# Adding up the routed expert rows: six weighted VectorE additions per token tile against ScalarE weighting and one VectorE sum

## What is computed

```python
x = x + attention(xn, Wq, bq, Wk, bk, Wv, bv, Wo, bo) + moe(xn, ...)

# attention: 16 heads of 128, causal, softmax in float32
# moe: 64 experts of capacity 128, each token goes to TOPK = 6 of them
scores = sigmoid(x_flat @ w_gate)
_, topk_idx = top_k(scores, 6)
w = take(scores, topk_idx); w = w / w.sum(-1)
out_r = (silu(g_r) * v_r) @ w_down          # per expert and slot
y_ts = out_r[flat_e, pos_c]                 # six rows of 256 per token
routed = (y_ts.reshape(N, 6, 256) * w[:, :, None]).sum(axis=1)
```

## Time and profile before

| | before |
|---|---|
| median of 3 runs | 2060.81 us (2058.49 to 2063.56) |
| the profiled execution, its own time | 2065.55 us |
| its span | 2063.8 us |
| PE busy | 1683.7 us, 82% of the span, 19016 instructions |
| DVE busy | 1502.6 us, 73%, 3148 instructions |
| ACT busy | 1090.3 us, 53%, 2300 instructions |
| POOL busy | 1101.2 us, 53%, 920 instructions |
| mean busy share of the 16 DMA engines in the slices of the attention parts | 5 to 7 tenths |

### The profile page before, as it was taken

The page is one execution under the profiler, slowest core; times in us unless marked ns, Lnnn a source line. Parts: engine busy times, 40 slices in busy tenths (PEclk is TensorE's granted clock), DMA queues, the critical chain, the costliest instruction groups (busy, mean ns, idle before and its releaser), DMA issues. The chain is left out here.

```text
span 2063.8 us, 49196 instructions
## 1 busy us (share of the span) xinstructions
PE 1683.7 (82%) x19016; PEld 1307.4 (63%) x19016; DVE 1502.6 (73%) x3148; ACT 1090.3 (53%) x2300; POOL 1101.2 (53%) x920
## 2 busy tenths in 40 slices
PE   1253089999999999999967788899899999888887
PEld 1242067777777777777756666677666666666665
DVE  5598956666667676666634478888888888888875
ACT  1520056666666666666622265555555555555564
POOL 0510046666666666666620066666666666666543
PEclk9676589999999999999977599999999999999999
DMA  5225067777665666656657566667666676667655
GB/s 182 102 102 196 0 129 135 134 136 129 123 110 104 123 103 101 105 103 104 109 130 218 171 112 121 119 120 147 120 122 121 117 139 120 122 119 144 118 90 109
DMA packets 695996, 253.35 MB, mean 123 GB/s; under 512 B 642384, under 2 KB 682145, under 8 KB 695008
## 3 DMA queue, kind: packets, MB, share of 16 engines
q1 hardware_dynamic: 668096, 204.12, 52.7%
q0 software_dynamic: 19232, 37.84, 7.2%
q10 hardware_dynamic: 8448, 8.39, 1.2%
HBM read 61.30 MB, written 54.66 MB: 56 GB/s over the span
## 5 line engine op out<-in xcount | busy, mean ns | idle before, releaser
L448 POOL TENSOR_TENSOR prob<-prob 128x128 f16<-128x128 f32 (+7 forms) x512 | 673.5, 1316 | 809.0 <-ACT prob L784 805.7
L777 ACT ACTIVATE prob<-prob,nmax 128x128 f32<-128x128 f32 (+7 forms) x512 | 398.0, 777 | 625.4 <-DVE prob L1135 568.0
L601 PE MATMUL ps_s<-kT,qT 128*128 128x512 f16 (+3 forms) x2304 | 460.6, 328 | 9.2 <-DVE prob L1135 5.7
L616 PE MATMUL ps_o<-probT,vh 128*128 128x256 f16 (+1 forms) x3840 | 434.4, 267 | 4.9 <-DMA probT<-prob 4.9
L1135 DVE TENSOR_SCALAR_CACHE_REDUCE prob<-ps_s,neg_scale 128x128 f32<-128x128 f32 (+7 forms) x512 | 408.8, 808 | 2.0 <-PE ps_s L603 1.8
L616 PEld LDWEIGHTS ps_o<-probT,vh 128*128 128x128 f16 x3840 | 372.0, 100 | 52.7 <-issue 5.8
L784 ACT CAST prob<-prob 128x128 f16<-128x128 f32 (+7 forms) x512 | 341.3, 667 | 2.9 <-DMA probT<-prob 0.6
L627 PE MATMUL ps_y<-wo,oT 128*128 128x256 f16 x1536 | 212.3, 275 | 126.5 <-DVE oT L1150 115.8
L601 PEld LDWEIGHTS ps_s<-kT,qT 128*128 128x128 f16 x2304 | 201.7, 99 | 162.9 <-issue 19.6
L567 PE MATMUL ps_t<-xT,wq 128*128 128x64 f16 x6144 | 195.2, 194 | 62.4 <-DMA xT<-xn_columns 61.0
L627 PEld LDWEIGHTS ps_y<-wo,oT 128*128 128x128 f16 x1536 | 136.2, 98 | 165.3 <-DVE oT L1150 136.7
(11 more groups left out here) (182 smaller groups left out, 1713.5 us busy)
## 6 DMA issues: line engine op xcount, KB each, us to landing
dispatched<-zeros SPq DMA_DIRECT2D x16, 512.0 KB, 5.4
probT<-prob SPq DMA_TRANSPOSE x512
ex<-dispatched SPq DMA_DIRECT2D x16, 512.0 KB, 4.3
expert_out<-eo ACTq DMA_DIRECT2D x16, 512.0 KB, 3.8
resid<-in_L_attn_x_dram SPq DMA_DIRECT2D x2, 2048.0 KB, 11.2
xn_rows<-xn SPq DMA_DIRECT2D x8, 512.0 KB, 3.0
xn_columns<-xnth SPq DMA_DIRECT2D x16, 256.0 KB, 2.3
xT<-xn_columns SPq DMA_DIRECT2D x8, 512.0 KB, 5.8
```

The lines of the kernel that those rows point to most:

```text
L448: pool.tensor_tensor(low_cols(j), prob_cols(j).rearrange("p (r k) -> p r k", k=P), high_cols(j), ALU.subtract).then_inc(p_low, 1)
L601: pe.matmul(s_cols(j, lo, hi), qT[:, u, a, j * P:(j + 1) * P], kT[:, u, c, lo:hi], start=(n == 0), stop=(n == 2 and hi < w))
L616: mm = pe.matmul(ps_o[:, lo:2 * P], vh[:, u, a, r * D:(r + 1) * D], probT[:, PT_AT[c] + 2 * r + s, lo:], start=(r + n == 0), stop=(r == 2 ...
L777: nc.scalar.activation(prob_cols(j), prob_cols(j), ACT.Exp, bias=nmax[:, j:j + 1], scale=-1.0, accum_out=rsum[:, i % 2, j:j + 1]).then_inc ...
```

## The change

The work of a tile is divided otherwise. `got` has a seventh row per buffer, which holds `cvec` and is written once. ACT multiplies each of the six gathered rows in place by its gate weight, two rows at a place, in three consecutive slots that begin 9 after the tile's first gather, each pair right after `softmax_exp`. DVE adds up the seven rows of the tile in one `tensor_reduce` over a view that has the rows innermost (slot 12 after the first gather), and adds the sum to `resid` at the next place. The gathers of tile `t` wait for the sum of tile `t - 2`, once per tile.

```diff
-        got = sb("got", [P, 2, TOPK, C])
+        got = sb("got", [P, 2, TOPK + 1, C])
+        mixed_rows = sb("mixed_rows", [P, C])
...
-        MIX_LAG = 12
+        RHYTHM = TOPK + 1
+
+        def tile_at(s, lag):
+            t, k = divmod(s - lag, RHYTHM)
+            return (t, k) if 0 <= t < NT else (-1, k)
+
...
             def gather(t, k):
-                if t > 1:
-                    pool.wait_ge(mix_step, (TOPK + 1) * (t - 2) + k + 1)
+                if t > 1 and k == 0:
+                    pool.wait_ge(mix_sum, t - 1)
...
+            def scale_rows(s):
+                t, n = tile_at(s, RHYTHM + 2)
+                if t < 0 or n > 2:
+                    return
+                if n == 0:
+                    act.wait_ge(gathered[t % 2], 16 * TOPK * (t // 2 + 1))
+                for k in (2 * n, 2 * n + 1):
+                    nc.scalar.activation(got[:, t % 2, k, :], got[:, t % 2, k, :], ACT.Copy,
+                                         scale=gate_w[:, t, k:k + 1]).then_inc(got_scaled, 1)
+
...
                     softmax_exp(i, 1)
+                    if mixing:
+                        scale_rows(TB * (i - i0) + 1)
                     high_v(i, 0)
...
-            def mix(t, k, added):
-                if k == 0:
-                    dve.wait_ge(gathered[t % 2], 16 * TOPK * (t // 2 + 1))
-                if t + k:
-                    dve.wait_ge(mix_step, (TOPK + 1) * t + k)
-                dve.wait_ge(y_added, added)
-                if k < TOPK:
-                    V.scalar_tensor_tensor(out=resid[:, t, :], in0=got[:, t % 2, k, :], scalar=gate_w[:, t, k:k + 1], in1=resid[:, t, :],
-                                           op0=ALU.mult, op1=ALU.add).then_inc(mix_step, 1)
-                else:
-                    V.tensor_tensor(resid[:, t, :], resid[:, t, :], cvec[:], ALU.add).then_inc(mix_step, 1)
+            def mix(s, added):
+                t, n = tile_at(s, RHYTHM + 5)
+                if t >= 0 and n == 0:
+                    dve.wait_ge(got_scaled, TOPK * (t + 1))
+                    if t:
+                        dve.wait_ge(mix_added, t)
+                    V.tensor_reduce(mixed_rows[:], got[:, t % 2, :, :].rearrange("p k c -> p c k"), AX.X, ALU.add).then_inc(mix_sum, 1)
+                if t >= 0 and n == 1:
+                    dve.wait_ge(mix_sum, t + 1)
+                    dve.wait_ge(y_added, added)
+                    V.tensor_tensor(resid[:, t, :], resid[:, t, :], mixed_rows[:], ALU.add).then_inc(mix_added, 1)
...
             attention(0, SPLIT, False)
+            dve.wait_ge(cvec_ready, 1)
+            for u in range(2):
+                V.tensor_copy(got[:, u, TOPK, :], cvec[:]).then_inc(bias_rows, 1)
+            dve.wait_ge(bias_rows, 2)
```

More of the change, by code:

```diff
@@ L475, in _ @@
                     low_probs(i, j)
-                    t, k = divmod(TB * (i - SPLIT) + j, TOPK + 1)
-                    if t < NT and k < TOPK:
+                    t, k = tile_at(TB * (i - SPLIT) + j, 0)
+                    if t >= 0 and k < TOPK:
                         gather(t, k)
@@ L805, in high_o, with attention @@
                 nc.scalar.activation(oT[:, c % 2, 0, :], ps_o[:, 0:2 * P], ACT.Copy, scale=O_SHIFT).then_inc(o_high, 1)
-            def attention(i0, i1):
+            def scale_rows(s):
[7 more added lines that the diff above has]
+                                         scale=gate_w[:, t, k:k + 1]).then_inc(got_scaled, 1)
+            def attention(i0, i1, mixing):
                 high_q(i0, 0)
@@ L816, in attention @@
                     softmax_exp(i, 0)
+                    if mixing:
+                        scale_rows(TB * (i - i0) + 0)
                     if old:
@@ L824, in attention @@
                     softmax_exp(i, 2)
+                    if mixing:
+                        scale_rows(TB * (i - i0) + 2)
                     if old:
@@ L828, in attention @@
                     softmax_exp(i, 3)
+                    if mixing:
+                        scale_rows(TB * (i - i0) + 3)
                     high_probs(i, 3)
                     softmax_exp(i, 4)
+                    if mixing:
+                        scale_rows(TB * (i - i0) + 4)
                     if more:
@@ L838, in attention @@
                     softmax_exp(i, 5)
+                    if mixing:
+                        scale_rows(TB * (i - i0) + 5)
                     if more:
@@ L842, in attention @@
                     softmax_exp(i, 6)
+                    if mixing:
+                        scale_rows(TB * (i - i0) + 6)
                     high_o(i, 0)
@@ L845, in attention @@
                     softmax_exp(i, 7)
+                    if mixing:
+                        scale_rows(TB * (i - i0) + 7)
                 high_probs(i1 - 1, 7)
@@ L850, in _ @@
             act.wait_ge(wscale_step, WSTEPS)
-            attention(0, SPLIT)
+            attention(0, SPLIT, False)
             def experts(g, first):
@@ L884, in _ @@
                 experts(g, False)
-            attention(SPLIT, B * H)
+            act.wait_ge(route_ready, 2)
+            attention(SPLIT, B * H, True)
         @block.vector
@@ L1187, in mix_at @@
                     def mix_at(j):
-                        n = TB * (i - i0) + j - MIX_LAG
-                        if mixing and 0 <= n < NT * (TOPK + 1):
-                            mix(n // (TOPK + 1), n % (TOPK + 1), NC * (i - 1) + j // 2)
+                        if mixing:
+                            mix(TB * (i - i0) + j, NC * (i - 1) + j // 2)
                     def mixed(j):
-                        return max(0, min(NT * (TOPK + 1), TB * (i - i0) + j - MIX_LAG + 1)) if mixing else 0
+                        return max(0, min(NT, (TB * (i - i0) + j - RHYTHM - 6) // RHYTHM + 1)) if mixing else 0
                     block_max(i, 0)
```

12 lines of the change are left out of this document (7 added, 5 removed).

## The result

| | before | after |
|---|---|---|
| median of 4 runs | 2059.74 us (2058.49 to 2063.56) | 2162.07 us (2160.3 to 2166.49) |
| the profiled execution, its own time | 2065.55 us | 2162.97 us |
| its span | 2063.8 us | 2161.2 us |

The ratio is 1.0497, with a 95% interval of 1.0475 to 1.0519: the change makes the kernel 102 us slower. The forecast was 89 us slower, 2150 with a range of 2100 to 2185, so the sign came as predicted and the time lies in the range.

What follows compares the result with a forecast made beforehand. A chain handed between DVE and ACT was taken as the bound. Per cycle of eight tiles 10.4 + 32.2 + 3.4 = 46.0 us against 23.8 removed, +22.2, times 4: 2060.8 + 89 = 2150 us, range 2100 to 2185.

Steps and rivals of the forecast that it cites:

- The chain: Second half of attention: DVE and ACT hand block_max, exponential, high and low part back and forth, some 24.0 us a step.
- the rival by which total work decides: Mixing steps: DVE's busy time decides, not its waits; steps fall to 24.3 us, 85 us less, 1975 us; chance 0.08.
- The 0.3 us that were taken off the quiet step for PE: Step without mixing: without PE's delays the chain takes some 24.0 us, 24.31 less 0.3.
- Removed, 23.8 us per cycle: Old mixing on DVE, held `yscale` included: 7 steps x 3.4 us saved per cycle of eight tiles; 4 cycles.
- The pairs on ACT, 10.4 per cycle: First and second weighted pair of a tile, ahead of the high part: 5.2 us each per cycle of eight tiles.
- The sum, 3.2 us: The seven-row sum on DVE: 2.02 us dense plus 1792 x 0.65 ns for the long step in the view.
- a free step (2.02): The strided sum on DVE takes only 2.02 us: 38 us less, 2112 us; chance 0.2.
- a full second pass (3.9): Every element of the sum takes a second 1.04 ns, 3.9 us: 22 us more, 2172 us; chance 0.12.
- What the sum waits for: DVE's sum waits for ACT's third pair behind block_max; wait and sum less present idle, 32.2 us per eight tiles.
- POOL holding the sum: DVE's sum is held by POOL's subtraction as `yscale` was: 16 us more, 2166 us; chance 0.06.
- The addition, 3.4 per cycle: Adding the sum to `resid` on DVE, once at each place per eight tiles, costs one step's present mixing, 3.4 us.
- the clock rival: PE: longer stalls bring twice as much lower-clock time, as much as now on the chain: 22 us more, 2172; chance 0.06.

Runs made afterwards that it cites:

- the bare kernel: The changed kernel with no mixing at all (no weighting, sum or additions; the gathers stay): 1991.05 us, 0.9649 of the kernel before.
- the two halves: The changed kernel with ScalarE's weighting alone, 2042.29 us, and with the sum and its addition alone, rows unweighted, 2063.36 us.
- the kernel with both edits: The changed kernel with the sum one place later and reading neighbouring floats (wrong elements added up): 2087.96 us, 1.0115 of the kernel before.
- the fastest version: The kernel before with six weighted additions per tile on DVE at chosen places, none ahead of `yscale`, constant row added in the first half: 1985.97 us.

## Why the prediction came right, and where its sizes were off

*The chain.* It held. The step without mixing and gathers takes 24.29 us with DVE at 69% and ACT at 65% of the stretch, and the rival by which total work decides (1975 us) fell: DVE lost work, and the step became 3.5 us longer. The 0.3 us that were taken off the quiet step for PE are there as waits, without mixing and gathers (1195 to 1980 us; in total, times, longest),

```profile
ACT oT L810 <- PE ps_o L621: 17.4, 34, 7.1
```

that is 0.3 us each but for the longest, but no run has a step under 24.29 except the last one, which has less to do. Since "before" and "after" were reckoned from the same 24.0, this cancels. How near PE itself, busy for 96% of that stretch, is to being the bound of the quiet step stays open; in the mixing steps of the two kernels it is at 82 and 89%.

*Removed, 23.8 us per cycle, 95 in all.* Measured by the bare kernel: 71. The term was 24 us too large: 16 are the gathers', which stay and show once their cover is gone, and the other 8 are the 0.3 us per step.

*The pairs on ACT, 10.4 per cycle, 42 in all for the first two.* The weighting took 493 ns, not 480. With all three pairs of each tile the run of ScalarE's weighting alone had 53 expected and gave 51.

*The sum, 3.2 us.* Measured 3.249, and 2.019 when dense. The long step thus costs 0.69 ns per element at 1024 bytes, next to 0.66 and 0.63 in the earlier trace rows for steps of 64 and 24 bytes. The rivals of a free step (2.02) and of a full second pass (3.9) both fell. By the rule cited from the Trainium skill (Advanced Engine Details and Errata, SBUF Cachelines) the strided read had to pay, and the trace agrees.

*What the sum waits for.* Forecast 1.5 to 2 us, released by ACT. Measured 48.1 us in all, 1.5 on average over the 32 sums: there are 28 waits, 1.57 us at place 3, 1.83 at place 0 (the row at 1548.40 below), and none at place 2. Taking the wait away gave 44 us, the coupling of the two halves 48; the forecast's terms, less the two halves as reckoned ahead of their runs, left 46.

*POOL holding the sum.* This rival fell in every one of the 32 sums, which take 3201 to 3310 ns whatever POOL does. In the row at 1548.40 below the sum runs 1.66 us beside a subtraction that takes its usual 2.12. The Trainium skill (SBUF — State Buffer, "SBUF: two separate sides") lets only VectorE instructions with two SBUF inputs, or in a two-port mode, contend with GpSimd: the trace agrees on both sides, with the sum free and the held L1146 and L1173 (lines of the kernel before) having two.

*The addition, 3.4 per cycle: mis-sized.* It held a `yscale` of about 2 us at place 1 to be paid. The rows, DVE and then POOL:

```profile
1548.40 3.23 DVE L1208 TENSOR_REDUCE mixed_rows<-got 128x256 f32<-128x1792 f32 x1 [1.83 <-ACT got L823]
...
1552.32 0.37 DVE L1212 TENSOR_TENSOR resid<-resid,mixed_rows 128x256 f32<-128x256 f32 x1
1552.62 0.43 DVE L1182 TENSOR_TENSOR yscale<-rinv,out_scale 128x8 f32<-128x8 f32 x1
```

```profile
1549.97 2.12 POOL L457 TENSOR_TENSOR prob<-prob 128x1024 f16<-128x1024 f32 x1 [1.35 <-ACT prob L793]
```

In the steps with the addition at place 1 the sum stands at place 0, and it delays DVE so much that POOL's subtraction has ended (1552.09) before `yscale` starts (1552.62). So it takes 0.40 or 0.43 in these four steps (why not 0.17 is not shown): 1.7 us per cycle, 7 in all, less than forecast.

*PE.* Left out of the sum, and the check on it failed: PE busy 82% of the stretch (579.53 of 710), not 75%. At 30.9 us a step that is 25.2 us of PE, where the quiet step has 23.1 (666.36 / 700 x 24.31), because more of it runs at the lower clock level: a granted 0.94 is 12% of the step at half speed, 3.7 us, which costs an estimated 1.9 of the 2.1 us more. The chain also waited for PE more often than before: the waits of ACT and DVE for PE in the mixing steps (1195 to 1980 us; in total, times, longest), after and before, are

```profile
ACT oT L814 <- PE ps_o L625: 5.9, 11, 0.8
ACT vh L807 <- PE ps_t L596: 4.0, 5, 1.1
DVE qf L1146 <- PE ps_t L576: 3.8, 9, 0.7
```

```profile
DVE qf L1110 <- PE ps_t L567: 0.9, 1, 0.9
DVE prob L1135 <- PE ps_s L603: 0.2, 1, 0.2
ACT oT L805 <- PE ps_o L616: 0.2, 1, 0.2
```

13.7 us against 1.3, some 12 us, where the clock rival had 22. That the clock is what brought these waits is not shown: the run with the sum one place later has the same granted 0.94 and only 5.6 us of them, and the bare kernel, at 1.00, has 20.9.

*The balance.* Per cycle the mixing cost 216.29 - 168 = 48.3 us where 46.0 were forecast, 9 us more in four cycles, and with the profiled execution 97 us slower than its counterpart against 89 forecast, that is about the whole of the difference. PE's 12 us more and `yscale`'s 7 less stand in it; the rest, some 4 us, is not assigned. Against the bare kernel the new mixing costs 171 us where 184 (4 x 46.0) were forecast, and the old 71 where 95 were. Both were too high, by 13 and 24 us, and only the 11 us between them reach the forecast difference: the mechanism was right, but that the time came so close is in part luck.

## What to carry to other kernels

Where two in-order engines hand a chain back and forth, busy shares say little: look in the timeline for the places where each waits for the other, and put extra work only there. A move to a half-idle engine still costs what lies between two links (here 0.6 us per us put on ACT), and a consumer placed right behind the instruction that its producer needs adds a wait on top; one place later takes it away. And look for small instructions with large mean times: a 128x8 one was held to the end of another engine's work, and moving one operation away from it gave 58 us. Look again after every edit: a shorter instruction ahead of it can bring the hold back, as in the kernel with both edits.

## What was not expected

- The indirect gathers cost 16 us (1991.05 against 1975.38) when nothing covers them, though no engine of the chain waits for their data; one step in 31 of the kernel with the gathers takes 27.85 us, the others at most 26.3.
- A hold by POOL depends on who starts when, to a tenth of a microsecond: in the run that puts `yscale` first, it starts 0.09 us before the subtraction and takes 0.17, and the operation that starts 0.01 us before it takes 2.42, to 0.29 after its end.
- Clock and time mostly moved together: the stretch with mixing was granted 0.94 in the changed kernel, 0.97 before and 1.00 in the fastest version, in all of which PE has the same work to do. The match is not strict (0.94 at 2118 us, 0.96 at 2113), and which of the two brings the other was not tried.
